# Splitting the experts' weights: eight by VectorE, none by GpSimd, and a drain of GpSimd where the last stage begins

## What is computed

```python
x = L0_attn_x                                    # [4, 1024, 256] f32
x = x + _layernorm(attn(_layernorm(x)))          # 16 heads of 64, causal
x = x + _layernorm(ffn(_layernorm(x)))
# ffn: rmsnorm(ln1), 16 heads of 16 with 4 kv heads, rope, causal attention, residual; then
h = _rmsnorm(x, ln2_w).reshape(-1, 256)          # T = 4096 tokens
rprobs = softmax(h @ gate_w.T)                   # 8 experts
topw, topi = top_k(rprobs, 2); topw = topw / sum(topw)
for e in range(8):                               # FFN = 512
    g = silu(h @ w13[e, :512].T) * (h @ w13[e, 512:].T)
    out = out + einsum('tf,hf->th', g, w2[e]) * wfull[:, e:e + 1]
return x + out
```

## Time and profile before

| | |
|---|---|
| median of the 3 runs | 2705.66 us |
| profiled execution: time, span | 2704.81 us, 2703.1 us |
| TensorE (PE) busy | 2348.3 us (87%) |
| VectorE (DVE) busy | 1705.7 us (63%) |
| ScalarE (ACT) busy | 1463.9 us (54%) |
| GpSimd (POOL) busy | 1055.0 us (39%) |
| software DMA queue q0 | 9216 packets, 18.96 MB |

### The profile page before, as it was taken

The page is one execution under the profiler, slowest core; times in us unless marked ns, Lnnn a source line. Parts: engine busy times, 40 slices in busy tenths (PEclk is TensorE's granted clock), DMA queues, the critical chain, the costliest instruction groups (busy, mean ns, idle before and its releaser), DMA issues. The chain is left out here.

```text
span 2703.1 us, 45876 instructions
## 1 busy us (share of the span) xinstructions
PE 2348.3 (87%) x12882; PEld 1428.3 (53%) x12882; DVE 1705.7 (63%) x4480; ACT 1463.9 (54%) x3225; POOL 1055.0 (39%) x1827
## 2 busy tenths in 40 slices
PE   4999999999999999999837599999999747999990
PEld 2556566555665556555523233333333545888870
DVE  5776763777556773677259677777776365444445
ACT  3566653666456663666338477777777443333332
POOL 0344442455344443455406222222222044555543
PEclk7999999999999999999869699999999867999995
DMA  3011010011001010011123311111110621111115
GB/s 105 17 29 29 25 44 15 19 29 45 25 19 29 25 44 15 19 29 29 27 70 160 105 35 35 35 35 35 35 35 18 207 90 51 52 52 52 52 46 189
DMA packets 141572, 135.56 MB, mean 50 GB/s; under 512 B 74400, under 2 KB 111008, under 8 KB 139680
## 3 DMA queue, kind: packets, MB, share of 16 engines
q1 hardware_dynamic: 132128, 113.84, 14.0%
q0 software_dynamic: 9216, 18.96, 2.4%
HBM read 87.58 MB, written 33.88 MB: 45 GB/s over the span
## 5 line engine op out<-in xcount | busy, mean ns | idle before, releaser
L288 POOL TENSOR_TENSOR a_A<-a_A,a_P 128x512 f32<-128x512 f32 (+3 forms) x320 | 316.0, 988 | 290.1 <-PE a_O L594 279.3
L1234 ACT ACTIVATE b_P<-b_SC 128x512 f32<-128x512 f32 (+3 forms) x768 | 328.9, 499 | 162.9 <-PE b_SC L1337 161.4
L442 ACT ACTIVATE a_P<-a_SC 128x512 f32<-128x512 f32 (+3 forms) x640 | 292.0, 469 | 202.6 <-PE a_SC L577 195.6
L500 DVE CUSTOM_DVE_ANT_0 a_MX<-a_MX,a_causal 128x128 f32<-128x128 f32 (+3 forms) x512 | 248.7, 502 | 154.9 <-PE a_MX L646 149.4
L576 PE MATMUL a_SC<-a_QR,a_KR 128*128 128x512 f32 (+3 forms) x768 | 318.4, 418 | 4.4 <-DMA a_QS<-a_minusT 2.9
L1176 POOL TENSOR_SCALAR_AFFINE_SELECT b_P<-b_P 128x128 f32<-128x128 f32 x512 | 146.2, 292 | 443.4 <-ACT b_P L1234 433.7
L1284 DVE CUSTOM_DVE_ANT_0 b_MX<-b_MX,b_causal 128x128 f32<-128x128 f32 (+3 forms) x512 | 248.7, 499 | 79.8 <-PE b_MX L1386 77.5
L646 PE MATMUL a_MX<-a_KR,a_QR 128*128 128x512 f32 (+3 forms) x768 | 282.9, 377 | 17.3 <-DVE a_peak L500 14.2
L1386 PE MATMUL b_MX<-b_K,b_Q 96*128 96x512 bf16 (+3 forms) x768 | 251.2, 339 | 42.8 <-ACT b_Q L1245 14.8
L327 POOL TENSOR_SCALAR_AFFINE_SELECT a_P<-a_P 128x128 f32<-128x128 f32 x448 | 143.8, 327 | 345.7 <-ACT a_P L442 342.3
L577 PE MATMUL a_SC<-a_QS,a_KS 65*128 65x512 f32 (+3 forms) x768 | 265.5, 350 | 0.0
(11 more groups left out here) (266 smaller groups left out, 4439.0 us busy)
## 6 DMA issues: line engine op xcount, KB each, us to landing
a_inv<-inv_rows SPq DMA_DIRECT2D x128, 128.0 KB, 2.9
stack_rows<-p_stk SPq DMA_DIRECT2D x32, 480.0 KB, 2.7
a_W<-in_w_pair SPq DMA_DIRECT2D x34, 384.0 KB, 3.7
b_stk<-stack_rows SPq DMA_DIRECT2D x136, 96.0 KB, 2.1
W<-in_w SPq DMA_DIRECT2D x8, 1024.0 KB, 7.4
c_E<-done_rows SPq DMA_DIRECT2D x8, 1024.0 KB, 6.8
n_x<-in_x SPq DMA_DIRECT2D x4, 1024.0 KB, 9.4
a_xT<-hold SPq DMA_DIRECT2D x4, 1024.0 KB, 4.8
```

The source lines that it names most:

```text
L288: eng.tensor_tensor(acc[h][c][:, a:], acc[h][c][:, a:], buffer(n, h)[:, a:], ALU.add).then_inc(added[h], 1)
L442: act.activation(buffer(n, h)[:, a:], SC[h][:, a:], ACT.Exp, scale=DH1 ** -0.5).then_inc(s["exp_done"], 1)
L500: dve.tensor_tensor_reduce(MX[c % MAX_BANKS1][:, 0:w], MX[c % MAX_BANKS1][:, 0:w], causal[:, BANK - w:], 1.0, 3 * NEG, ALU.add, ALU.max, p ...
L1234: act.activation(probs[k % RING2][:, a:], SC[k % SCORE_BANKS][:, a:], ACT.Exp, scale=DH2 ** -0.5).then_inc(s["exp_done"], 1)
```

## The change

Of the split, GpSimd's part goes. VectorE's loop is written out in Python (`for g in range(NG)`), and in trips 3, 4, 5 and 6 it splits experts 4, 0, 1 and 2 between its additions and its wait for the squares, each whole expert in one copy and one subtraction of 2048 columns. Expert 3 follows behind the loop. ScalarE rounds 5 and 6 in routing and 7 in `experts`; VectorE subtracts for these three in `experts`. W13 is loaded in the order 4, 0, 1, 2, 3, 5, 6, 7, and SyncE waits, before the second, third and fourth pair, for the pair before. One counter, `rest_ready`, stands for the two on which TensorE waited. In `combine` GpSimd starts with a drain.

```diff
-BY_POOL, BY_ACT, LAST_ROUNDED = (0, 1, 2, 4), (3, 5, 6), 7
-BY_DVE = BY_ACT + (LAST_ROUNDED,)
-CHUNK = 512
+SPLIT_IN_LOOP, SPLIT_NEXT, BY_ACT, LAST_ROUNDED = {3: 4, 4: 0, 5: 1, 6: 2}, 3, (5, 6), 7
+LOADS = (4, 0, 1, 2, 3, 5, 6, 7)
...
             for g in range(1, NG - 1):
                 stage_in(g)
                 keep(g - 1)
-                for e in ((2 * g - 2, 2 * g - 1) if 2 * g <= EXPERTS else ()):
-                    load(e)
+                if 2 * g <= EXPERTS:
+                    if g > 1:
+                        sp.wait_ge(w13_in, 32 * (g - 1))
+                    for e in LOADS[2 * g - 2:2 * g]:
+                        load(e)
...
-            pool.wait_ge(w13_in, 16 * EXPERTS)
-            for x, e in enumerate(BY_POOL):
-                done = min(NG, 2 * e + 2) if e < EXPERTS // 2 else 0
-                pool.wait_ge(s["h_ready"], 4 * done)
-                pool.wait_ge(s["summed"], 4 * done + 1)
-                for n in range(0, KD * 2 * FFN, CHUNK):
-                    cols = slice(n, n + CHUNK)
-                    pool.tensor_copy(of_expert(W13R, e)[:, cols], of_expert(W13, e)[:, cols]).then_inc(rounded_by_pool, 1)
-                    pool.wait_ge(rounded_by_pool, (x * KD * 2 * FFN + n) // CHUNK + 1)
-                    rest_of(pool, W13, W13R, W13S, e, cols).then_inc(rest_by_pool, 1)
...
                 four = bass.ds(g * 4, 4)
+                if g in SPLIT_IN_LOOP:
+                    split_w13(SPLIT_IN_LOOP[g])
                 dve.wait_ge(s["summed"], g * 4 + 5)
...
-            with dve.Fori(0, NG) as g:
+            def split_w13(e):
+                x = LOADS.index(e)
+                dve.wait_ge(w13_in, 32 * (x // 2 + 1))
+                if e < EXPERTS // 2:
+                    dve.wait_ge(s["summed"], 8 * e + 9)
+                dve.tensor_copy(of_expert(W13R, e), of_expert(W13, e)).then_inc(rounded_by_dve, 1)
+                dve.wait_ge(rounded_by_dve, x + 1)
+                rest_of(dve, W13, W13R, W13S, e).then_inc(rest_ready, 1)
+
+            for g in range(NG):
                 first(g)
+            dve.wait_ge(s["h_ready"], NT)
+            split_w13(SPLIT_NEXT)
...
-            pe.wait_ge(rest_by_pool, len(BY_POOL) * KD * 2 * FFN // CHUNK)
-            pe.wait_ge(s["rest_by_dve"], len(BY_DVE))
+            pe.wait_ge(rest_ready, EXPERTS)
...
-            for x, e in enumerate(BY_DVE):
+            for x, e in enumerate(BY_ACT + (LAST_ROUNDED,)):
                 dve.wait_ge(rounded, x + 1)
-                rest_of(dve, W13, W13R, W13S, e).then_inc(s["rest_by_dve"], 1)
+                rest_of(dve, W13, W13R, W13S, e).then_inc(rest_ready, 1)
...
         @block.gpsimd
         def _(pool):
+            pool.drain()
             for t in range(NT):
                 pool.wait_ge(s["y_ready"], t + 1)
```

More of the change, by code:

```diff
@@ L1470, in round_w13, with rest_of @@
     return act.activation(of_expert(W13R, e), of_expert(W13, e), ACT.Copy)
-def rest_of(eng, W13, W13R, W13S, e, cols=slice(None)):
-    return eng.tensor_tensor(of_expert(W13S, e)[:, cols], of_expert(W13, e)[:, cols], of_expert(W13R, e)[:, cols].bitcast(F32),
-                             ALU.subtract)
+def rest_of(eng, W13, W13R, W13S, e):
+    return eng.tensor_tensor(of_expert(W13S, e), of_expert(W13, e), of_expert(W13R, e).bitcast(F32), ALU.subtract)
 def route(nc, hold, norm_z, shift_z, A2, scratch, w_out, ln2, w_gate, h_rows, share_rows, source, target, expert_of, W13, W13R, W13S,
-          w13, w13_in, rounded, rounded_by_pool, rest_by_pool, W2, w2, w2_in, ident):
+          w13, w13_in, rounded, rounded_by_dve, rest_ready, W2, w2, w2_in, ident):
     rows = hold.rearrange("p b k s -> p (b k s)").rearrange("p (t d) -> p t d", d=D)
@@ L1952, with experts @@
 ROWS_HELD = 5
-def experts(nc, h_rows, share_rows, done_rows, source, target, W13, W13R, W13S, rounded, rest_by_pool, W2, w2_in, ln2, expert_of, ident, spare):
+def experts(nc, h_rows, share_rows, done_rows, source, target, W13, W13R, W13S, rounded, rest_ready, W2, w2_in, ln2, expert_of, ident, spare):
     with ExitStack() as ctx:
@@ L1972, in experts @@
         names = ("ln_in", "turned", "hR_ready", "hS_ready", "gu_ready", "gated", "act_ready", "at_ready", "actT_ready",
-                 "y_ready", "y_copied", "folded", "rest_by_dve")
+                 "y_ready", "y_copied", "folded")
         s = dict(zip(names, spare))
@@ L2264, in layer @@
             rounded = inner.enter_context(nc.semaphore("w13_rounded"))
-            rounded_by_pool = inner.enter_context(nc.semaphore("w13_rounded_by_pool"))
-            rest_by_pool = inner.enter_context(nc.semaphore("w13_rest_by_pool"))
+            rounded_by_dve = inner.enter_context(nc.semaphore("w13_rounded_by_dve"))
+            rest_ready = inner.enter_context(nc.semaphore("w13_rest_ready"))
             ident = inner.enter_context(nc.sbuf_tensor("ident", [P, P], F32))
@@ L2270, in layer @@
             route(nc, hold, norm_z, shift_z, A2, large[:, NT * D:], w_out2, ln2, w_gate, h_rows, share_rows, source, target,
-                  expert_of, W13, W13R, W13S, w13, w13_in, rounded, rounded_by_pool,
-                  rest_by_pool, W2, w2, w2_in, ident)
-            experts(nc, h_rows, share_rows, done_rows, source, target, W13, W13R, W13S, rounded, rest_by_pool, W2, w2_in, ln2, expert_of,
+                  expert_of, W13, W13R, W13S, w13, w13_in, rounded, rounded_by_dve,
+                  rest_ready, W2, w2, w2_in, ident)
+            experts(nc, h_rows, share_rows, done_rows, source, target, W13, W13R, W13S, rounded, rest_ready, W2, w2_in, ln2, expert_of,
                     ident, spare[12:])
```

## The result

The changed kernel takes 2683.77 us (median of 6 runs, 2679.38 to 2688.75) beside 2705.89 us (6 runs) for the kernel before: ratio 0.9920, 95% interval 0.9908 to 0.9932. It is faster by 22 us, against 13.2 forecast, and it lies under the range. In the medians further down, two slow executions each of e8_no_pacing (2720 and 3925 us) and e5_gpsimd_busy (4305 and 7088 us) are left out. The profiled execution took 2687.63 us for a span of 2685.6, 17.5 us under the span of before.

| stretch | before | after | difference |
|---|---|---|---|
| start to routing's first Z | 2110.93 | 2110.66 | -0.3 |
| first Z to the reading of the logits | 93.28 | 83.66 | -9.6 |
| logits to the first hS | 50.54 | 48.40 | -2.1 |
| first hS to GpSimd's last addition | 439.18 | 439.51 | +0.3 |
| from there to the end of the span | 9.17 | 3.37 | -5.8 |

What follows compares the result with a forecast made beforehand. It took GpSimd's closing drain to bound the end, TensorE the experts' stage, and no full engine routing's loop, with its VectorE-ScalarE ring. Loop 5.2 + experts' start 2.1 + drain 5.9 = 13.2 us off 2705.66: 2692.5, named 2692; range 2686 to 2699.

Steps and rivals of the forecast that it cites:

- The drain: Last stage: an early GpSimd drain pays the software DMAs' 8.9 us while idle; closing barrier 5.9 us sooner, bounds 0 and 5.9.
- The experts' start: Start of experts' stage: VectorE does three subtractions, not four, before hS; 2.1 us less.
- The split: VectorE's routing loop: copy 1.2 us, subtraction 2.29, 3.6 with handover; costs 0 to 0.1 us per trip in the waits.
- SyncE's pacing: SyncE's wait before each pair of W13 loads in routing: cost 0, bounds -0.6 and +3 us.
- the fifth: Split behind routing's loop: its 3.6 us fit VectorE's 4.96 us wait for the logits.
- Rival D: VectorE's longer loop code stalls on instruction fetches: one stall leaves 3 us gain, from two on slower, 2713; chance 0.04.
- VectorE's loop written out ... I count 0: Routing's early trips: fixed code gains 0, bounds 0 and 1.2 us, as ScalarE is ready only 0.3 us before VectorE.
- the sum for trips 6 and 7: End of routing's loop without GpSimd's pieces: HN of trip 7 starts at 2192.4, not 2197.63; 5.2 us less.
- I let TensorE reach 2177.5 as before: Routing, before trip 5's HN turn: TensorE, delayed by r_stage's DMA and the lower clock, gets there no sooner.
- Rival A: Routing's loop: clock doesn't fall in trip 5, the ring alone sets the pace; routing 10.6 us early, 2687.1; chance 0.17.

Runs made afterwards that it cites:

- e8_no_pacing: Kernel after without SyncE's waits for the pair before, each pair of experts having its own semaphore; 2681.75 us, 0.9930 of the kernel before.
- e5_gpsimd_busy: Kernel after with GpSimd doing 16 copies and 16 subtractions of 128x512 that nobody reads; 2691.24 us, 0.9959 of the kernel before.
- e7_gpsimd_queue: Kernel after with W13's loads issued by GpSimd on its software queue instead of by SyncE; 2679.37 us, 0.9913 of the kernel before.
- e2_written_out_only: Kernel before with only VectorE's routing loop written out in Python, GpSimd still splitting four experts; 2701.40 us, 0.9985 of the kernel before.
- e1_drain_only: Kernel before with one GpSimd drain added at the start of the last stage (combine); 2698.55 us, 0.9980 of the kernel before.

## Why the prediction was wrong in size

- **The drain: right.** 5.8 in the trace, 5.9 alone (1.6 to 9.2 by its interval). The first drain behind the experts' stage is long and the next is not. That software DMAs make it long was inferred from one trace; the 0.7 us that eight of them add to routing's drain (e7_gpsimd_queue) bear it out, but what GpSimd does in the 8.9 us is not shown.
- **The experts' start: right**, 2.1 us.
- **The split: right.** Copy 1.22, subtraction 2.29, hidden in the waits, and the fifth inside the wait for the logits (1.82 us left of 4.96).
- **SyncE's pacing: right**, nothing. Rival D did not show: no gap without a wait in the written-out code.
- **"VectorE's loop written out ... I count 0": the step that failed.** Its premise was that ScalarE is ready only 0.3 us ahead of VectorE, so that no more than this could be gained. But ScalarE's readiness is no fixed time. It waits for HN through TensorE; when all four HN come in 1.14 us, directly behind the reciprocal, TensorE turns them in one go and ScalarE reads them in 1.57 us in place of 1.82. The idle 0.50 before HN is labelled with the reciprocal as its releaser and is 0.04 in fixed code: it was the loop's register work, not a dependency. Together a trip without waits for DMAs is 7.7 and not 9.35 - 0.3. The same step is in the sum for trips 6 and 7, which takes HN and Z as fixed code but keeps 4.43 and 3.64 us of register code from the squares to HN. They measured 3.69 and 2.88, and from HN of trip 6 to the squares it was 3.06, not 3.6: 2.0 us.
- **"I let TensorE reach 2177.5 as before": 2175.0.** TensorE's turn, which waits for `r_stage`, began 1.95 us sooner than before, and its project took 5.90 us, not 6.73. With only the loop written out (e2_written_out_only) that turn begins 52.7 us behind the first Z, after 53.6, before 55.3; this speaks for the faster trips as the cause, and single traces don't show it. HN of trip 6 starts at 2181.8, not at the 2185.2 of the sum: 3.4 us. Trip 7 takes 5.94 us, not 7.24: 1.3 us. So HN of trip 7 starts at about 2187.8, not 2192.4. These 4.6 us, 2.5 of TensorE and 2.0 of register code left in the sum, are the miss of the profiled execution (17.5 - 13.2 = 4.3); the other terms together are off by 0.3.
- **Rival A was underpriced.** The clock does fall or not, even in the same kernel: the second trace lost one fall and 6.8 us. I gave A 10.6 us for the loop, because I left the old, slow ring in it. The loop of before took 93.3 us (96.9 in the trace of e1_drain_only). With one fall ahead of the last trip it takes 76.9 (the kernel after again), 16.4 us less than 93.3, and with none 71.7 (one load a trip), 21.6 less. The first trace of the kernel after had two.
- The medians are 22.1 us apart, the times of the two profiled executions 17.2. The 4.9 us between are not traced: the clock's fall in attention one (3.6 us), which comes in some executions of either kernel's code, and the second fall in the loop have about the right size, but no trace of a run near the median was taken. This part of the miss stays open.

## What to carry to other kernels

In a ring of engines, an engine that seems just ready may be so because it waits for the one that is sped up: walk the ring once around with the new durations before calling a gain capped. Idle time that is labelled with a releaser on the same engine, or with "issue", inside a register loop is suspect; compare it with the same operations in fixed code. And where a DMA queue is full for a few trips, spread the loads over all trips: here it took the time from 0.9920 to 0.9892 of that before and the loop from 76.9 or 83.7 to 71.7 us, and making two more engines' loops faster on top of it brought nothing more. Last, take a second trace of the same kernel before sharing out a few microseconds: here two traces of one loop differed by as much as the shares.

## What was not expected of the hardware

TensorE's granted clock differs between executions of the same code: 0.53 or 1.00 over the same 38 matmuls near the end of attention one, worth 3.6 us. In the loop a wait of 1.4 us for a DMA was followed by a fall in one trace (a project of 6.21 us in place of 3.70), and in another the fall came only behind the next wait, of 2.10 us. GpSimd's drain behind the 216 software DMAs of the experts' stage took 8.885 us to the nanosecond in ten traces, 8.878 in that of e7_gpsimd_queue and 8.887 in that of e5_gpsimd_busy.
